# Two-layer decoder on one core: low halves as jobs of their own, steps of the normalisations spread out, projections laid between the links of chains

## What is computed

```python
x = x + attn(ln(x))            # 16 heads of 8, softmax over 256 keys          "attn0"
x = x + cross(ln(x), ctx)      # 8 heads of 64, 512 context tokens of 96       "cross0"
x = x + mixer(ln(x))           # 16 heads of 8, tokens in two classes          "mixer"
    # sim = mean over heads of cos(q, q_g); classes: rescaled sim > 0.9;
    # each token attends to its class, the first 5 (registers) to both
x = x + delta(ln(x))           # state <- state*(1 - b*kk) + b*v*k, scanned over 256 tokens,
    # out = state.q; then layer norm, gate silu(x Wg), projection
x = x + cross(ln(x), ctx)      # 16 heads of 64                                "cross1"
x = x + feed(ln(x))            # ternary weights, gelu, layer norm
# cross: softmax((x Wq)(ctx Wk)^T / 8) (ctx Wv), then Wout and a bias
```

## Time and profile before

| | |
|---|---|
| median of 3 runs | 511.52 us (510.71 to 512.24) |
| profiled execution: its own time | 510.47 us |
| profiled execution: span | 508.6 us |
| PE busy | 382.5 us (75%) |
| DVE busy | 279.5 us (55%) |
| ACT busy | 209.6 us (41%) |
| POOL busy | 124.6 us (25%) |
| mean granted TensorE clock | 0.853 of full |

### The profile page before, as it was taken

One profiled execution on the slowest core, in us unless ns is written; L12 is line 12 of the kernel. 1 busy time (PEld: TensorE's weight loads), 2 busy tenths in 40 slices (PEclk: granted clock), 3 DMA queues, 4 the chain that ended last, 5 costly groups with the idle time before them and its releaser, 6 DMA issues. The chain is left out here.

```text
span 508.6 us, 7128 instructions
## 1 busy us (share of the span) xinstructions
PE 382.5 (75%) x2667; PEld 210.4 (41%) x2667; DVE 279.5 (55%) x579; ACT 209.6 (41%) x360; POOL 124.6 (25%) x118
## 2 busy tenths in 40 slices
PE   2687697989878896978847575686779798769734
PEld 1453333435545432435425234343345464335423
DVE  3674534646573445564345644797773836753332
ACT  2265346445351542553534332253344424734230
POOL 5000000336360000000011500168544424443400
PEclk9999879989897896998767867598897988988875
DMA  7500000010000000000100000000000000000000
GB/s 217 125 2 0 2 1 1 1 41 1 1 3 0 0 1 0 1 3 2 43 0 1 0 1 1 0 1 1 1 1 1 0 1 2 1 0 12 2 0 10
DMA packets 9655, 6.14 MB, mean 12 GB/s; under 512 B 3723, under 2 KB 8726, under 8 KB 9622
## 3 DMA queue, kind: packets, MB, share of 16 engines
q1 hardware_dynamic: 9622, 5.69, 4.3%
HBM read 5.39 MB, written 0.26 MB: 11 GB/s over the span
## 5 line engine op out<-in xcount | busy, mean ns | idle before, releaser
L1201 DVE TENSOR_REDUCE mxw<-PS 128x2 f32<-128x1024 f32 x48 | 58.5, 1221 | 20.0 <-PE PS L614 19.9
L532 POOL TENSOR_TENSOR Psum<-Pc 128x512 f32<-128x512 f32 x24 | 31.2, 1298 | 116.0 <-ACT Pc L978 115.5
L978 ACT ACTIVATE Pc<-PS 128x1024 f32<-128x1024 f32 x48 | 49.1, 1022 | 24.0 <-PE PS L642 22.5
L670 PE MATMUL ACC<-Pc,V 128*64 128x256 f32 x384 | 58.3, 430 | 0.0
L1198 DVE TENSOR_REDUCE mx<-PS 128x4 f32<-128x1024 f32 x32 | 38.9, 1223 | 23.1 <-PE PS L607 23.0
L534 POOL TENSOR_TENSOR Psum<-Psum,Pc 128x512 f32<-128x512 f32 x24 | 31.0, 1290 | 57.6 <-ACT Pc L978 57.4
L978 ACT ACTIVATE Ps<-PS 128x1024 f32<-128x1024 f32 x32 | 32.6, 1021 | 9.5 <-PE PS L626 8.7
L670 PEld LDWEIGHTS ACC<-Pc,V 128*64 128x64 f32 x384 | 25.4, 148 | 25.6 <-issue 18.2
L759 PE MATMUL PS<-ctxT,wk_c 96*128 96x512 f32 x48 | 30.1, 759 | 6.2 <-ACT V L1033 2.6
L546 POOL TENSOR_TENSOR mid<-mid 128x256 f32<-128x256 f32 x2 | 1.5, 726 | 130.8 <-ACT mid L1081 130.8
L1216 DVE TENSOR_TENSOR Zs<-ACC,Zs 128x256 f32<-128x256 f32 x24 | 10.2, 424 | 38.4 <-ACT Zs L1000 38.4
(11 more groups left out here) (271 smaller groups left out, 752.3 us busy)
## 6 DMA issues: line engine op xcount, KB each, us to landing
Qm<-mrow SPq DMA_DIRECT2D x64, 0.5 KB, 1.7
wq_c<-in_c_Wq_dram SPq DMA_DIRECT2D x1, 512.0 KB, 5.7
spread<-in_c_Wo_dram SPq DMA_DIRECT2D x1, 512.0 KB
Pc<-in_ctx_dram SPq DMA_DIRECT2D x1, 384.0 KB, 4.2
wk_c<-in_c_Wk_dram SPq DMA_DIRECT2D x1, 384.0 KB, 6.6
wv_c<-in_c_Wv_dram SPq DMA_DIRECT2D x1, 384.0 KB, 7.6
csth<-in_const_dram SPq DMA_DIRECT2D x1, 320.0 KB, 4.9
x<-in_x_dram SPq DMA_DIRECT2D x2, 128.0 KB, 2.3
```

What stands on the lines that cost most here:

```text
L532: alone(v.tensor_tensor(t, p[:, :, 0, :], p[:, :, 1, :], ALU.add), "sums_done")
L670: last = mm(ACC[64 * e:64 * e + 64, c % 2, 0:S], V[:, b * 4 + kt, (2 * u + e) * 64:(2 * u + e + 1) * 64], Pc[:, 2 * (c % 2) + i, (2 * e + ...
L978: e = A(to, src.rearrange("p a c -> p (a c)"), ACT.Exp, scale=PHASES[name].scale)
L1201: last = v.tensor_reduce(to, src, AX, ALU.max)
```

## The change

1. The low halves of keys and queries are jobs of their own, K2 and Q2, on DVE only; K and Q keep the part of PE and ACT. K2 or Q2 stands right behind the K or Q, or behind the M of the same step.
2. The order within a step becomes turn, S, div, norm, mask, V, K, Q, prep, M, K2, Q2, PV, dT, den, and then all other jobs. Before, S stood ahead of turn, div and norm stood at the end, Q and prep behind everything.
3. norm and div of a unit move from step 2k+3 to 2k+4; Q from 2k-6 to 2k-8. A part of `attentions` has a fourth number, `late`: S of cross0 and of cross1, b = 1, come two steps later, so that two steps before them hold no S.
4. `negm` has three buffers.
5. Jobs placed by hand get other steps. In `classes`: V:y000 now stands ahead of the output of cross0, b = 1; V:y050 and the first four K of cross1 leave the stretch ahead of the first S of the mixer and go to steps 10 to 16 of the mixer (K:y000 ahead of M:m131, K:y010, V:y050, K:y020, K:y030). The jobs simT and cls stand directly ahead of prep:m000, where before V:y030 to V:y050 stood between. rt:m100 stands ahead of dg and dn instead of behind them. In `ends`, V:y070 stands ahead of oT, K:y070 ahead of dout. In `three`, the four sp of b = 1 stand at steps -4, -2, 0, 2 instead of -1 to 2; tg, tt, bt stand one to three steps further behind what they wait for.

No instruction is added or removed on any engine.

```diff
-WITHIN = ("S", "turn", "mask", "M", "PV", "dT", "den", "div", "norm", "put", "prep", "Q")
+WITHIN = ("turn", "S", "div", "norm", "mask", "V", "K", "Q", "prep", "M", "K2", "Q2", "PV", "dT", "den")
...
-            put(2 * k - 5, 1, "M", 0)
-            put(2 * k - 4, 2, "M", 1)
-            put(2 * k - 3, 3, "turn")
...
-            for kind, step, i in (("PV", 1, 0), ("PV", 2, 1), ("den", 3, 0), ("norm", 3, 0)):
-                put(2 * k + step, never, kind, i)
...
+                put(s - 8, "Q", 0, 0)
+                put(s - 8, "Q2", 0, 0)
+            put(s - 5, "M", 0, 1)
+            put(s - 4, "M", 1, 2)
+            put(s - 3, "turn", 0, 3)
+            for step, kind, i in ((0, "S", 0), (1, "S", 1), (1, "PV", 0), (2, "PV", 1), (3, "den", 0), (4, "norm", 0)):
+                put(s + step, kind, i)
...
-    one = attentions((a0, 0, -9), (a0, 1, -3), (x0, 0, 12), (x0, 1, 20))
+    one = attentions((a0, 0, -9, 0), (a0, 1, -3, 0), (x0, 0, 14, 2), (x0, 1, 22, 2))
...
-        3: [K0[0]], 6: [K0[1]], 8: [K0[2]],
-        9: [zT, V0[0]], 10: [out] + ln + [V0[1]], 11: ln2 + [V0[2]] + xt, 12: [K0[3]],
-        17: [zT_], 18: [out_] + ln_, 19: ln2_ + [V0[3]] + xt_,
-        25: cross_tail(x0, 0) + mln, 26: mln2, 27: mxt, 28: mix[:2], 29: mix[2:3], 31: mix[3:]})
+        3: K0[0], 6: K0[1], 8: K0[2], 10: [zT], 11: [out] + ln + V0[0], 12: ln2 + V0[1] + K0[3], 13: xt + V0[2],
+        18: [zT_], 19: [out_] + ln_ + V0[3], 20: ln2_, 21: xt_,
+        29: cross_tail(x0, 0) + mln, 30: mln2, 31: mxt, 32: [qt, sim], 33: [kq], 34: [vs], 35: [simT]})
...
-    classes = cross_tail(x0, 1) + ln + V1[0:2] + ln2 + xt + [qt, sim, kq, V1[2], simT, vs, job("cls", f0)] + V1[3:5]
+    classes = V1[0] + cross_tail(x0, 1) + ln + V1[1] + V1[2] + ln2 + xt + [qt, sim, kq, vs] + V1[3] + [simT, job("cls", f0)]
...
-        -9: [V1[5]], -6: K1[0:1], -4: K1[1:2], -2: K1[2:3], -1: K1[3:4],
-        1: [qx], 3: [rs], 7: [rt], 9: [rv, zT], 10: [out, qx_] + ln, 11: ln2 + [rs_], 12: xt, 13: [dp], 14: [dg, dn, rt_],
-        16: [dt], 17: [s0]})
-    ends = [rv_, zT_, s1, K1[4], s2, out_] + ln_ + [V1[6], s3, K1[5], oT, dl] + ln2_ + xt_ + [dl2, K1[6], yT, V1[7], dout] \
-        + ln4 + [K1[7]] + ln24 + xt4
+        -8: V1[4], 1: [qx], 3: [rs], 7: [rt], 10: [rv] + K1[0], 11: [zT, qx_], 12: [out, rs_] + ln + K1[1], 13: ln2 + V1[5], 14: xt,
+        15: [dp, rt_] + K1[2], 16: [dg, dn] + K1[3], 18: [dt]})
+    ends = [rv_] + [s0] + K1[4] + [zT_, s1] + V1[6] + [out_] + ln_ + [s2] + K1[5] + [s3] + ln2_ + V1[7] + xt_ + [oT, dl] + K1[6] \
+        + [dl2, yT] + K1[7] + [dout] + ln4 + ln24 + xt4
...
-    three = attentions((y1, 0, -9), (y1, 1, 11))
+    three = attentions((y1, 0, -9, 0), (y1, 1, 13, 2))
...
-        -6: [dp], -4: [dg, dn], -2: [dt], -1: [s0], 0: [s1], 1: [s2], 2: [s3], 4: [oT], 5: [dl], 6: [dl2],
-        7: [yT], 8: [dout] + ln, 9: ln2, 10: xt,
-        13: [job("gsum")], 14: [job("tg")], 15: tern[:1], 16: [job("tt")], 18: cross_tail(y1, 0) + ln_, 19: ln2_, 20: xt_,
-        21: tern[1:], 22: [job("tt", i=1)], 23: [ff1], 24: [job("bt"), fl], 25: [fl2], 26: [fT], 28: [ff2]})
+        -9: [dp], -8: [dg, dn], -5: [dt], -4: [s0], -2: [s1], 0: [s2], 2: [s3], 4: [oT], 5: [dl], 6: [dl2],
+        8: [yT], 9: [dout], 10: ln, 11: ln2, 12: xt,
+        14: [job("gsum")], 16: [job("tg")], 17: tern[:1], 20: cross_tail(y1, 0) + ln_ + [job("tt")], 21: ln2_, 22: xt_ + tern[1:],
+        24: [ff1, job("tt", i=1)], 25: [fl], 26: [fl2], 27: [fT], 28: [job("bt")], 29: [ff2]})
...
-        negm = sb("negm", [P, 2, S], F16)
+        negm = sb("negm", [P, 3, S], F16)
...
-                elif kind == "K":
-                    src = arrived(j)
-                    dve.wait_ge(sem("k_high"), nth[j])
+                elif kind == "K2":
+                    k = job("K", name, b, u)
+                    src = arrived(k)
+                    dve.wait_ge(sem("k_high"), nth[k])
```

More of the change, by code:

```diff
@@ L75, in prepare, with put @@
     return job("prep" if PHASES[name].small else "Q", name, b, p)
-WITHIN = ("S", "turn", "mask", "M", "PV", "dT", "den", "div", "norm", "put", "prep", "Q")
+WITHIN = ("turn", "S", "div", "norm", "mask", "V", "K", "Q", "prep", "M", "K2", "Q2", "PV", "dT", "den")
 def attentions(*parts):
[L86 to L91, removed]
+    units = [(name, b, u, start, late) for name, b, start, late in parts for u in range(PHASES[name].U)]
+    steps = {s: [] for s in range(-10, 2 * len(units) + parts[-1][3] + 3)}
+    for k, (name, b, u, start, late) in enumerate(units):
+        s = 2 * k + late
+        def put(step, kind, i=0, first=None):
+            if first is not None:
+                step = max(step, start + first + 2 * u, -10)
+            steps[step].append(job(kind, name, b, u // 2 if kind in ("Q", "Q2", "prep") else u, i))
@@ L92, in attentions @@
         if PHASES[name].small:
             if u % 2 == 0:
[L94 to L98, removed]
+                steps[max(s - 9, start + u, -10)].append(job("prep", name, b, u // 2))
+            put(s - 7, "mask", 0, 1)
+            put(s - 5, "M", 0, 2)
+            put(s - 4, "M", 1, 3)
@@ L99, in attentions @@
+            put(s - 3, "turn", 0, 4)
+            for step, kind, i in ((0, "S", 0), (1, "S", 1), (2, "PV", 0), (3, "dT", 0), (4, "div", 0)):
+                put(s + step, kind, i)
         else:
             if u % 2 == 0:
-                steps[max(2 * k - 6, start + u, -10)].append(job("Q", name, b, u // 2))
-            put(2 * k - 5, 1, "M", 0)
-            put(2 * k - 4, 2, "M", 1)
-            put(2 * k - 3, 3, "turn")
-        for i in range(2):
-            put(2 * k + i, never, "S", i)
@@ L122, in place_in, with within @@
     for s, js in jobs.items():
-        steps[s][1].extend(js)
+        steps[s] += js
 def line(steps):
-    return [j for s in sorted(steps) for part in steps[s] for j in part]
+    def within(j):
+        return WITHIN.index(j[0]) if j[0] in WITHIN else len(WITHIN)
+    return [j for s in sorted(steps) for j in sorted(steps[s], key=within)]
 def norm_jobs(n, b):
@@ L641, in scores @@
                         r = slice(64 * e, 64 * e + 64)
-                        last = mm(dst[:, e, :], one_row[r, :], negm[r, c % 2, :].unsqueeze(1).to_broadcast([64, 2, S]),
+                        last = mm(dst[:, e, :], one_row[r, :], negm[r, c % 3, :].unsqueeze(1).to_broadcast([64, 2, S]),
                                   start=False, stop=True)
@@ L988, in _ @@
                     else:
-                        A(negm[:, c % 2, :], src[:, 0, 0:S], ACT.Identity, scale=-1.0).then_inc(freed(j), 1)
+                        A(negm[:, c % 3, :], src[:, 0, 0:S], ACT.Identity, scale=-1.0).then_inc(freed(j), 1)
                 elif kind == "PV" and PHASES[name].small:
```

32 lines of the change are left out of this document (13 added, 19 removed).

## The result

The changed kernel took 494.28 us (median of 4 runs, 492.36 to 495.85), the kernel before 511.12 beside it (4 runs): ratio 0.967, 95% interval 0.962 to 0.971. That is 16.8 us faster, inside the range of 464 to 505, but 14.3 short of the forecast 480; the gain was about half of the one forecast. Beside the experiments some executions fell into a slower state, and the ratios leave these out.

What follows compares the result with a forecast made beforehand. The prediction took PE's list as the bound: its work, 126 us of idle time, and half speed. Its terms summed to -32 us from 511.5, giving 480 us (473 to 492, chance 0.50), with an overall range of 464 to 505.

Steps and rivals of the forecast that it cites:

- (a): Low halves in attn0, less two waits at turn early in cross0: net -2.5 us, bounds +1 and -6.
- (b): Cross0: normalisation and norm gaps close, -7.5; turn ahead of S costs +4; net -3.5 us, bounds +1 and -11.
- (c): Classes and mixer: first S 15.5 us earlier, mixer pays net +5.5; sum -10, bounds -3 and -16.
- (d): Delta block: first half -1 us, bounds +3 and -4; second half -3.5, bounds 0 and -6.
- (e): Cross1: gaps closed 12 us, steps without S open +3.5; net -8.5, bounds -2 and -18.
- (f): Half speed avoided on PE behind closed gaps in attn0, cross0 and cross1: 3 us taken, of 12 at most.
- Rival 1: Half speed goes with the gaps, so more time is saved: 468 us (460 to 473), chance 0.20.
- (g): The tails, from 474 us on: same jobs, same order, 0.
- Rival 2: Turn ahead of S costs every unit of cross attention a 1.2 us wait: 504 us (492 to 510), chance 0.19.
- Rival 3: The cross-unit loop becomes the bound: norm held by POOL, turn waits 2.1 us in 24 units; 526 us, chance 0.07.
- Rival 4: Nothing moves: each closed gap reappears at the next wait of an in-order engine; 511 us, chance 0.04.

Runs made afterwards that it cites:

- e2_norm_back: The changed kernel with norm and div moved back to step 2k+3 and to the end of the step: 502.12 us, ratio 0.977 to the kernel before.
- the control: The changed kernel once more, nothing altered, on the chip of the last four runs: 495.09 us, ratio 0.968 to the kernel before.
- e1_s_first: The changed kernel with S ahead of turn in each step, as it was before the change: 484.89 us, ratio 0.944 to the kernel before.
- e4_cover_cls: The changed kernel with V:y030, V:y040 and V:y050 behind simT and cls, ahead of prep:m000: 487.07 us, ratio 0.948 to the kernel before.
- e5_k_back: The changed kernel with the first four K and K2 of cross1 back ahead of the mixer's first S: 491.54 us, ratio 0.958 to the kernel before.
- e6_k2_first: The changed kernel with K2 and Q2 ahead of M in a step instead of behind it: 501.47 us, ratio 0.978 to the kernel before.
- e7_ends: The changed kernel with ln2:130 ahead of K:y050 and sp:030, and xt:130 ahead of V:y070, in delta b = 0: 491.27 us, ratio 0.957 to the kernel before.

## Why the prediction was right, and where it was not

The sign and the range were right, the size was off by half. By its own steps:

- **(a)** -2.5, came -4.0. The wait of dT for the low half is 2.54 as worked out. My 2.9 us for two waits at turn, at the start of cross0, were too much: 1.0 (turn:c010) was left, and none longer before one of 1.48 at 110.98.
- **(b)** -3.5, came -3.4. The gaps at xt and out:c000 are gone, and three waits of 1.5 to 1.6 us stand at turn instead (1.2 forecast). But the reason given for xt, norm a step later, is refuted: `e2_norm_back` has norm back and no such gap in cross0. (The four gaps of this step add up to 8.0 us, not 7.5.) So the size is in part luck.
- **(c)** The step that failed most. Right were the transpose of sim (161.82 against 174.09, 4.9 us earlier beyond the 7.4 of (a) and (b), 5.2 forecast) and the class chain's gap (4.61). Wrong was the term of 18.7 us from prep to the first S: I had summed it nearly all at full speed, with a gap of 4.4 us directly ahead of it that I had put there myself. It took 25.15, and with PE kept at work in that gap 18.9 and 19.5, so the length of the chain was right and its clock wrong: +6.4. The length was partly luck: the terms named for it add up to about 17.4, with 3.8 for the second prep too, and V:y040, which stands between, is not among them. The mixer paid 7.2 instead of 5.5, with 1.4 left of the 6.6 us at rt:m100, and 5.3 ahead of dt (5.8 forecast).
- **(d)** First half -1, came +3.1, at the edge of its bound; 2.1 of it are idle time of PE (15.6 before, 17.7 now) and 1.1 busy time. Waits of 2.63, 3.34 (POOL, ahead of oT) and 2.57 us (xt:130) of before became one of 6.76 at xt:130, a little less in all. New is one of 4.46 us ahead of yT:

```profile
279.10 1.27 DVE L1375 TENSOR_TENSOR_SCAN scratch<-scratch 128x256 f32<-128x256 f32 x2 [0.15 <-DVE scratch L1364]
280.60 1.18 DVE L1169 SCALAR_TENSOR_TENSOR rt<-rt 128x2 f32<-128x2 f32 x1
282.02 1.97 DVE L1175 TENSOR_SCALAR xn<-x,mv,rstd 128x128 f32<-128x128 f32 x2
284.05 0.69 PE L583 MATMUL PS<-cst,xn 128*128 128x128 f32 x2 [6.76 <-DVE xn L1175]
...
286.86 0.20 ACT L959 ACTIVATE rstd<-rt 128x2 f32<-128x2 f32 x1
289.74 1.23 DVE L1247 TENSOR_TENSOR small_kv<-PS,small_kv 128x1024 f16<-128x1024 f32 x1 [3.15 <-ACT small_kv L1026]
293.04 0.69 PE L583 MATMUL PS<-cst,wo_c 128*128 128x128 f32 x2 [4.46 <-DVE wo_c L1388]
```

  ln2 of tile 130 stood behind the last sp and its scans in the old list too; what changed there is PE's cover, for K:y050, oT and dl stood between and now only V:y070 does. dl2, which yT waits for, has its root from ACT at 287.06 but stands in DVE's queue behind K2:y060, which waits for ACT's copy; it starts at 290.88, 3.8 us later. In the kernel before it stood ahead of that low half and yT waited for nothing. I had named this order and that of K2:y070 ahead of dout's addition (a wait of 4.62 us at xt:040, 3.61 before), but taken both as paid for by V:y070. No run puts dl2 ahead of K2:y060, so this reading rests on the trace. Second half -3.5, came -2.8: the first three pairs of scans take 1.27 each, the fourth 2.78.
- **(e)** -8.5, came -9.8. The four waits of the earlier trace rows are gone or down to 0.4; the loop with turn ahead of S, which I had called small, has 2.1, 1.1 and 2.4 us at single units.
- **(f)** -3 of half speed. PE's busy time fell by 10.3 us, so speed gave more than I took for it, while idle time gave 5.0, where most of the other 29 had been meant to come from. Rival 1 was right that clock and gaps go together, but at turn and ahead of prep new gaps took speed back, and 468 was far off. The sign that I had set for this step, a mean clock above 0.87, didn't come: it is 0.862. The Trainium skill ("TensorE: Matmul & The Clock Gate", section "What's actually happening") says that throttled is the default and that activity releases it. The tail agrees (32.2 us against 25.0 with unused work in the waits); the start of the mixer agrees only in part, below.
- **(g)** 0, came +3.0. "Same jobs, same order" is no reason for the same time: the two waits ahead of out:y100 are the same in both kernels (1.57 and 2.18 us before, 1.56 and 2.18 after), but before, its sixteen matmuls took 3.40 and then 2.05 us, and now 3.78 both times. From out:y100 to the end PE is idle 14.4 us in both; the 3.0 us are busy time alone (14.8 and 17.8). With the code of the tail unchanged it took 32.1 to 32.2 us in the changed kernel, the control and three others, 30.9 in `e1_s_first`, and 29.3 to 29.4, about as in the kernel before (29.2), in `e4_cover_cls`, `e5_k_back`, `e6_k2_first` and `e7_ends`. So the length of the tail depends on something ahead of it, and up to 3 us of a difference between two kernels may be that; what decides it is open.

**Rival 2** (504) named the right mechanism. Its place in the sum was 4 in cross0 and at most 3.5 in cross1; `e1_s_first` prices it at 9.4. The bound of 15 us for the waits at these maxima, which I had set as a sign of a wrong prediction, was passed with 16.5 (the view puts 10.9 of it to "issue", as in the wait at 124.50). **Rival 3** (526) did not come: norm's last instruction in cross1 takes 703 ns (701 before). **Rival 4** was half right: the waits at turn are 22.7 us longer, while PE's idle time fell by only 5.0.

The miss is 480 against 494.3, or in the profile -15.3 against -32: 8.6 of it in (c), 4.1 in the first half of (d), 3.0 in the tail, 3 in (f) as a separate term; the rest nearly cancels.

Not settled: what the change's remaining parts (steps of tg, tt and bt, rt ahead of dn, the sp spread out) are worth each, since only norm's step (7.8), the order of the low halves (7.2), turn (-9.4) and the place of K (nothing gained) were tried by themselves.

## What to carry to other kernels

When an engine's list is reordered, sum its busy time before and after as well as its gaps: here two thirds of the gain, and over half of the miss (6.4 us ahead of the mixer, 3.0 in the tail), was the clock. The stretch behind the bare gap of 4.6 us began at half speed in every kernel that had it, and in six of them stayed there to the first S; such a stretch is better costed at half speed until something shows otherwise. In a queue that is walked in order, put what is ready (S) ahead of what waits for another engine (turn), unless somebody is late for the latter. And of a moved job ask both what it no longer stands behind and what it now stands behind: yT of the delta block (behind K2:y060), the class chain and turn all lost what the same edit had won elsewhere.

## What the runs showed of the hardware that was not expected

- **Half speed without a pause.** In the changed kernel PE ran from 166.81 to 180.87 with no gap, on small float16 matmuls and one projection, and stayed at half speed all that time (0.42 us for a 128x256, V at 3.78). With V3 to V5 ahead it ran from 160.75 without a gap; the granted clock was 0.50 from 162.0 to 165.4, 1.00 to 172.2 and 0.50 again behind it (0.28, then 0.36, then eight of L604 at 1.89 instead of 1.05). So in these two kernels being busy in the profile was not enough to get or to keep full speed. Why isn't shown; nothing was tried on it.
- **Unused work pays.** Thirteen unused matmuls of 96x512 in the waits of the last tail made the kernel 7.6 us faster; five ahead of the mixer 4.4; ten there, longer than the wait, nothing. In these places PE had been waiting anyway.
- **DVE held by GpSimd.** L1169 on 128x2 elements takes 0.29 us on average and 1.18 in the rows above, ending at 281.78; a tensor_tensor of POOL on 128x512 ran from 280.51 to 281.77. The next two (L1175, 1.97 for two, 0.52 each on average) ran beside a second one from 281.85 to 283.11. The fourth pair of scans, 2.78 instead of 1.27, is of the same kind. The Trainium skill ("SBUF — State Buffer", section "Terms") calls the port pair of DVE and GpSimd an exclusive lock for the whole instruction; these rows agree with it, at 0.9 us for L1169 and 1.4 for the two L1175 (a pair at 301.95, with POOL idle, took 0.60).
- **A small matmul at half speed isn't twice as long.** The first prep matmul takes 0.27 at full and 0.37 to 0.42 us at half speed, V 1.88 and 3.78. These lengths overlap; from one group of four such matmuls of prep to the next it is 0.64 us at full and 1.07 at half speed.
